# Which engine corrects the softmax probabilities: a quarter of the corrections from GpSimd to ScalarE, with the order of all work planned again

## The reference, cut to what matters

```python
x = x + attn_a(layernorm(x), W_K, W_Q, W_V, W_O)      # changed
x = x + ffn(layernorm(x), ...)
x = x + attn_b(layernorm(x), ...)
x = x + ffn(layernorm(x), ...)

def attn_a(x, W_K, W_Q, W_V, W_O):                     # 16 heads of 64, 2048 rows
    K, Q, V = (einsum('bpd,ihd->biph', x, W) for W in (W_K, W_Q, W_V))
    scores = einsum('biph,biqh->biqp', K, Q)           # causal mask
    attn = softmax(scores / sqrt(64), axis=-1)
    z = einsum('biph,biqp->biqh', V, attn)
    return z_flat @ W_O.T
```

## Time and profile before

| | before |
|---|---|
| median of three runs | 1415.31 us (1414.78 to 1417.1) |
| the profiled execution | 1417.41 us, its span 1415.6 us |
| PE busy (share of the span) | 1195.6 us (84%) |
| POOL busy | 1036.4 us (73%) |
| DVE busy | 883.9 us (62%) |
| ACT busy | 791.7 us (56%) |
| mean granted TensorE clock | 0.943 of full speed |

### The profile page before, as it was taken

One profiled execution on the slowest core, in us unless ns is written; L12 is line 12 of the kernel. 1 busy time (PEld: TensorE's weight loads), 2 busy tenths in 40 slices (PEclk: granted clock), 3 DMA queues, 4 the chain that ended last, 5 costly groups with the idle time before them and its releaser, 6 DMA issues. The chain is left out here.

```text
span 1415.6 us, 24422 instructions
## 1 busy us (share of the span) xinstructions
PE 1195.6 (84%) x7936; PEld 856.5 (61%) x7936; DVE 883.9 (62%) x1948; ACT 791.7 (56%) x2192; POOL 1036.4 (73%) x973
## 2 busy tenths in 40 slices
PE   5899999999999999999999999999975394886375
PEld 4666666666667667666666676676654392443275
DVE  5666666756675675668566666757644163998354
ACT  5667576756657675767566576756642162222143
POOL 0788878979997988889799979878891453553333
PEclk9999999999999999999999999999996595998588
DMA  4940200200020001002000200010000121000023
GB/s 119 133 122 4 57 1 1 55 7 1 1 60 1 1 16 46 1 1 60 1 1 1 61 1 1 16 45 1 1 1 1 47 64 49 1 0 1 22 60 97
DMA packets 52689, 41.18 MB, mean 29 GB/s; under 512 B 14177, under 2 KB 41442, under 8 KB 52578
## 3 DMA queue, kind: packets, MB, share of 16 engines
q1 hardware_dynamic: 50018, 34.50, 11.1%
q0 software_dynamic: 2560, 5.26, 1.1%
HBM read 13.49 MB, written 9.48 MB: 16 GB/s over the span
## 5 line engine op out<-in xcount | busy, mean ns | idle before, releaser
L320 POOL TENSOR_SCALAR at_prob<-at_prob,at_scale 128x512 f32<-128x512 f32 (+3 forms) x640 | 865.0, 1372 | 5.6
L348 DVE TENSOR_REDUCE at_nmax<-at_ps 128x1 f32<-128x512 f32 (+3 forms) x640 | 374.9, 605 | 206.5 <-PE at_ps L508 203.1
L423 ACT ACTIVATE at_prob<-at_ps,at_nmax 128x512 f32<-128x512 f32 (+3 forms) x640 | 392.2, 623 | 32.1 <-DVE at_nmax L348 31.7
L517 PE MATMUL at_ps<-ident,at_prob 128*128 128x128 f32 x2176 | 336.4, 277 | 70.4 <-POOL at_prob L320 53.8
L517 PEld LDWEIGHTS at_ps<-ident,at_prob 128*128 128x128 f32 x2176 | 252.3, 140 | 177.8 <-POOL at_prob L320 99.9
L437 ACT ACTIVATE at_probT<-at_ps 128x512 f32<-128x512 f32 (+1 forms) x288 | 165.1, 573 | 256.3 <-PE at_ps L517 253.2
L505 PE MATMUL at_ps<-at_k_st,at_q_parts 128*128 128x512 f32 (+3 forms) x640 | 281.7, 440 | 3.5 <-ACT at_prob L423 1.3
L532 PE MATMUL at_ps<-at_probT,at_v 128*64 128x256 f32 (+1 forms) x2304 | 270.1, 374 | 7.0 <-DVE at_probT L371 6.9
L371 DVE COPY at_probT<-at_ps 128x512 f32<-128x512 f32 (+1 forms) x288 | 189.4, 658 | 125.7 <-PE at_ps L517 124.4
L508 PE MATMUL at_ps<-at_k_st,at_q_parts 128*128 128x512 f32 (+3 forms) x640 | 252.5, 395 | 0.0
L532 PEld LDWEIGHTS at_ps<-at_probT,at_v 128*64 128x64 f32 x2304 | 154.9, 136 | 107.8 <-issue 47.9
(11 more groups left out here) (188 smaller groups left out, 1269.7 us busy)
## 6 DMA issues: line engine op xcount, KB each, us to landing
at_q_parts<-at_q_parts SPq DMA_DIRECT2D x64, 256.0 KB, 3.5
f_xs<-slots_in SPq DMA_DIRECT2D x48, 64.5 KB
slots_in<-zeros SPq DMA_DIRECT2D x2, 1536.0 KB, 16.8
wall<-in_L_ffn_w_dram SPq DMA_DIRECT2D x1, 2048.0 KB, 17.9
wall<-in_L_ffn_w_dram SPq DMA_DIRECT2D x4, 512.0 KB, 6.2
f_got<-slots_out SPq DMA_DIRECT2D x8, 256.0 KB, 3.7
out_dram<-x SPq DMA_DIRECT2D x4, 256.0 KB, 2.3
slots_out<-f_ys,f_back POOLq DMA_INDIRECT x48
```

What stands on the lines that cost most here:

```text
L320: pool.tensor_scalar(cols, cols, scale[:, k, u, c:c + 1], None, ALU.mult).then_inc(s_fix, 1)
L348: dve.tensor_reduce(nmax[:, j % 2, u % 4, c:c + 1], bank, AX.X, ALU.max, negate=True).then_inc(s_max, 1)
L423: act.activation(prob[j % 2][u % 4][:, c * BANK:c * BANK + w], ring[use_of["score", p, u, c] % RING][:, 0:w], ACT.Exp, bias=nmax[:, j % 2, ...
L517: last = pe.transpose(turn_ps[h][:, b * P:(b + 1) * P], prob[j % 2][2 * i + h][:, t * P:(t + 1) * P], ident[:, :])
```

## The change

The correction with h = 1 and i = 1 goes to ACT, as a copy with a scale taken from the same column of factors; the other three stay on POOL. The plan gets new lengths for `fix`, `fix` gets a place in ACT's ranking (behind `factor` and `leave`, ahead of `evict`, `vproject`, `high` and `exp`), a `turn` comes after both its fixes by name, and there is a semaphore for each engine's fixes. Since lengths, engines and ranks are changed, the order of every engine is another one.

```diff
+    def fixer(h, i):
+        return "act" if h == 1 and i == 1 else "pool"
...
-                    step(("fix", p, j, c, h, i), "pool", 0.2 + 1.0 * w, ("pool", "scale", p, j), last)
+                    length = {"pool": 0.28 + 1.28 * w, "dve": 0.1 + 0.5 * w, "act": 0.2 + 0.45 * w}[fixer(h, i)]
+                    step(("fix", p, j, c, h, i), fixer(h, i), length, ("pool", "scale", p, j), last)
...
-                step(("turn", p, j, h, g), "pe", 0.44 * w, ("pool", "fix", p, j, 2 * g // TPC, h, 1))
+                step(("turn", p, j, h, g), "pe", 0.44 * w,
+                     *[(fixer(h, i), "fix", p, j, 2 * g // TPC, h, i) for i in range(2)])
...
-              "act": ["factor", "leave", "evict", "vproject", "high", "exp"],
+              "act": ["factor", "leave", "fix", "evict", "vproject", "high", "exp"],
...
+                    elif kind == "fix":
+                        _, _, j, c, h, i = it
+                        k, u, w = j % 2, 2 * i + h, width(4 * j + 2 * i + h, c)
+                        act.wait_ge(s_scale, STEPS * p + j + 1)
+                        cols = prob[k][u][:, c * BANK:c * BANK + w]
+                        act.activation(cols, cols, ACT.Copy, scale=scale[:, k, u, c:c + 1]).then_inc(s_fix["act"], 1)
...
-                        pe.wait_ge(s_fix, count_of["pool", "fix", p, j, 2 * g // TPC, h, 1])
+                        for i in range(2):
+                            e = fixer(h, i)
+                            pe.wait_ge(s_fix[e], count_of[e, "fix", p, j, 2 * g // TPC, h, i])
```

More of the change, by code:

```diff
@@ L182, in attention_plan @@
         running = [(t, s) for t, s in running if t > now]
-    return order, row, chunks, width, turned, run_of
+    return order, row, chunks, width, turned, fixer, run_of
 def attention(nc, shp, keep, x_in, w_k, w_q, w_v, w_o, fetch):
@@ L191, in attention @@
     STEPS = NT // 2
-    order, row, chunks, width, turned, run_of = attention_plan(PAIRS, NT, NC, TPC)
+    order, row, chunks, width, turned, fixer, run_of = attention_plan(PAIRS, NT, NC, TPC)
     uses = [it for it in order["pe"] if it[0] in ("score", "project", "vproject", "out")]
@@ L260, in attention @@
         s_low, s_gap, s_factor, s_part, s_total, s_rinv = (sem(n) for n in ("s_low", "s_gap", "s_factor", "s_part", "s_total", "s_rinv"))
-        s_scale, s_fix = sem("s_scale"), sem("s_fix")
+        s_scale, s_fix = sem("s_scale"), {e: sem("s_fix_" + e) for e in ("pool", "act")}
         s_turn = [sem(f"s_turn{h}") for h in range(2)]
@@ L319, in _ @@
                         cols = prob[k][u][:, c * BANK:c * BANK + w]
-                        pool.tensor_scalar(cols, cols, scale[:, k, u, c:c + 1], None, ALU.mult).then_inc(s_fix, 1)
+                        pool.tensor_scalar(cols, cols, scale[:, k, u, c:c + 1], None, ALU.mult).then_inc(s_fix["pool"], 1)
             @block.vector
```

## The result

| | before | changed |
|---|---|---|
| median | 1415.84 us (1414.78 to 1417.1, 4 runs) | 1371.43 us (1368.79 to 1372.22, 4 runs) |
| ratio to before | 1 | 0.9683 (95% interval 0.9666 to 0.9700) |
| profiled execution | 1417.41 us, span 1415.6 | 1372.22 us, span 1370.5 |

The change saves 44 us, 3.2%. The forecast was 1365, a gain of 50, in a range from 1335 to 1396.

The account below looks back on a forecast made before the run. PE was taken to bound attention, stopped by POOL's throughput. From the profiled 1417.4 us, -60 + 15 - 5 = -50 gave 1367.4, hence 1365 for the median, in a range of 1335 to 1396.

Parts of the forecast that it names:

- What bounds the kernel: In attention, 57 to 1042 us: PE carries it, 93% busy; POOL's throughput makes it wait, taken as 65 us.
- Rival D: Attention's chain max, exp, weigh, total, scale: POOL's lateness is all latency, the wait is renamed; no change, 1415 us; 4%.
- Counts and prices: Attention's corrections: 160 of 640 move; POOL loses 227 us, ACT gains 103 at 688 ns per wide one.
- The body: Attention from 57 to 1042 us: 60 of 65 us of PE's wait on POOL goes, 15 us is given back.
- Rival B: Attention's weight loads: all their lost time returns, up to 87 us plus 5 to 8 at the end; 1335 us; 15%.
- The orders are new everywhere: All engines' lists: a longer planned POOL fix lets PE take other work first; no gain of its own counted.
- ACT's slack: ACT in attention, 57 to 1042 us: rises from 66% to 76 or 80% busy, below PE, work beside other work, not free.
- rival A: ACT in attention becomes the late one; 35 to 45 us given back, gain 20 to 30, 1385 to 1395 us; 20%.
- My charge of 15 us: ACT fixes ahead of evictions: one in four of 160 delays PE by half its length, 14 us; bounds 0 and 60.
- The tail: The 29 us behind 1042 us: three POOL fixes a chunk, PE about 5.4 us a chunk; gain 5, bounds 1 and 8.
- 2 us for an earlier scale: After the last exp: weigh and scale stood behind the previous pair's fixes; with POOL free, 2 us go.
- Rival C: ACT's list stops on POOL's late scale in each of 64 row pairs; 27 us slower, 1442 us; 6%.

Follow-up runs that it names:

- doubled kernel: Changed kernel in its own order, each correction on ACT preceded by a plain copy of the same columns onto themselves: 1442.96 us, ratio 1.0190.

## Why the prediction was right or wrong

**What bounds the kernel: right.** PE carries attention, and it was POOL's throughput in the wide row pairs that stopped it. Rival D (a wait that takes another name) fails for the change, and is just what the kernel with only the length changed shows.

**Counts and prices: right, with one low and one total high.** POOL was to fall to about 810 us and fell to 812.8. For a wide correction on ACT I took the exp's 688 ns from the earlier trace rows; it takes 717, and the narrow one 504. The Trainium skill (ScalarE: Activation LUTs, What ACT_TABLE_LOAD costs) came closer with an estimate of 706 and 492. The trace agrees roughly with its 93 ns for a per-row operand too: the doubled kernel's copy without one took 623 ns and with one 723.

ACT's busy time rose by 89.0 us, to 880.7, not by my 103 to 895, although the records of its corrections add up to 107. The instruction behind a wide one mostly starts 0.63 us after it, so the records overlap, and busy time counts the overlap once.

**The body: right in its sum, in part by luck.** I had 60 back and 15 given away, 45; the last exp came 41.4 us earlier. No run shows the two terms apart. And the same move gave 18 us with the old length in the plan and 34 in before's order, both under the 35 to 65 of my forecast. The 44 needed an order made with the true length, and on the new orders I had put nothing. PE's wait on POOL did go (2.3 us left), and the evictions took 27.7 instead of 21.4. The weight loads' own wait on POOL fell by 81 us (98.7 to 17.8 within attention) and PE's by 51, and the kernel got 44 faster, nearer to the lower bound. Rival B, that the loads' idle time comes back, falls. The Trainium skill (Perfetto Trace Analysis, Identifying the Most-Contended Engine) reads nearness to the limit from the weight loads, beside the share of peak arithmetic. In the kernel with one-column corrections and their plan they were busy 605 of 843 us, 72%, with PE at 98.7%: by that share there would still be room where hardly any gap was left between matmuls.

**The step that was wrong:** "The orders are new everywhere ... I put no gain of its own on that." Beside before's order with the move it happened to bring only 11 us here. Yet the move is worth 18 us with the old length in both plans, 55 with the true one in both, 34 in before's order and 95 in the new one, and the new order alone is 50 us worse than the old. My sum took the move's worth to be a property of the work; it is one of the work and the order together.

**ACT's slack: wrong in size.** I named ACT's 80% under rival A and still let its work lie beside the rest, as if most of the last fifth were free. The change itself stayed short of A, but at 78% ACT stood close to the 80.5% that no kernel here passed, some 25 us of work in 913, and the next 93 us cost 71.5, with some 20 of them the experiment's own at most. My charge of 15 us isn't confirmed as such: what the runs give is 7.7 us for all corrections in this order, and 10 us for having chosen ACT instead of DVE, the latter with another plan.

**The tail: right.** 4.4 us against 5, a chunk 5.35 us against "about 5.4", and from the last scale to the last leave 25.2 us against "some 25". Of the 2 us for an earlier scale only 0.7 came: weigh was free to start at once (997.67, by POOL's timeline), but scale then waited 2.33 us for `total`, which stood behind a copy of `probT` in DVE's list, and came 2.8 us behind the last exp's end, where it had been 3.5. The shorter chunks made up for it.

**Rival C (slower):** ACT's corrections waited for scale 4.8 us in all, 16 times, so its condition never arose.

## What to carry to other kernels

Where orders are planned, price a move by two further builds: the old order with the work moved, and the new order with it moved back. The first tells what the engine's relief is worth, the second whether the new order can stand without it. A wait on a step is no measure of what that step costs once orders are made to hide it; taking the step out with a new plan is (43 us here, against 8 with the order kept and 2.3 in the waits). And when an engine is relieved, spread the work by what each receiver can still take: a quarter each on ACT and DVE gave 20 us more than half on DVE or a quarter on ACT, and 10 more than a quarter on DVE.

## What was unexpected of the hardware

With a quarter of the corrections on DVE, those on POOL got slower: 1614 ns on average instead of the 1564 of the earlier trace rows. The longest took 1852 instead of 1573 ns, and DVE's own went from 335 (a narrow one) to 929, by the views of the two lines:

```profile
L325 POOL TENSOR_SCALAR at_prob<-at_prob,at_scale x480: 593/1559/1852, 39.2 to 1007.4; 128x512 f32<-128x512 f32 x96, 128x128 f32<-128x128 f32 x32, 128x384 f32<-128x384 f32 x32
```

```profile
L383 DVE TENSOR_SCALAR at_prob<-at_prob,at_scale x160: 335/487/929, 39.8 to 993.2; 128x512 f32<-128x512 f32 x128, 128x256 f32<-128x256 f32 x32
```

Each view gives the shortest, median and longest. In the changed kernel, with those on ACT, POOL's longest was 1573. The timeline separates the cases. Here DVE's second and fourth take 0.92 us instead of 0.48 or 0.49, and POOL's five take 8.29 us where five took 7.72 in the earlier trace rows:

```profile
502.80 0.48 DVE L383 TENSOR_SCALAR at_prob<-at_prob,at_scale 128x512 f32<-128x512 f32 x1 [0.33 <-POOL at_scale L318]
502.86 8.29 POOL L325 TENSOR_SCALAR at_prob<-at_prob,at_scale 128x512 f32<-128x512 f32 x5
...
504.74 0.92 DVE L383 TENSOR_SCALAR at_prob<-at_prob,at_scale 128x512 f32<-128x512 f32 x1
...
506.16 0.49 DVE L383 TENSOR_SCALAR at_prob<-at_prob,at_scale 128x512 f32<-128x512 f32 x1
...
508.10 0.92 DVE L383 TENSOR_SCALAR at_prob<-at_prob,at_scale 128x512 f32<-128x512 f32 x1
```

Counted over that trace, 187 of POOL's 320 wide corrections ran beside none of DVE's, and none of these took over 1568 ns; the 133 that did took 1690 on average. With half of the corrections on DVE, 14 of DVE's 256 wide ones ran beside none of POOL's and took at most 490 ns; the others took 641 on average and up to 962. So the two slow each other down, and not every time. The Trainium skill (GPSIMD Engine Reference, Key points) says that POOL shares its SBUF interfaces with VectorE; these rows fit that. What it costs the kernel isn't measured; with it, the kernel was still 10 us faster than with ACT.
